# Small VectorE results in PSUM, and fills issued earlier, in the first stage of a four-layer kernel

## The reference

```python
# x = x + tanh(g_xattn[0]) * mix(layernorm(x), ctx, ctx, Wt, Wp, Wg, Wz, gamma, beta)
t = einsum('oc,bcd->bod', Wt, inp_v)          # inp_v = ctx
p = einsum('oc,bcd->bod', Wp, inp_q)          # inp_q = layernorm(x)
g = einsum('oc,bcd->bod', Wg, inp_k)          # inp_k = ctx
att = einsum('bgcd,bgcd->bg', pg, gg) * 0.125 # one number per batch row and group of 16 channels
x = einsum('goc,bgcd->bgod', Wz, att * tg)
xn = (x - mean) / sqrt(var + EPS)             # over the 16 channels and 256 columns of a group
return xn * gamma + beta + inp_v
```

## Time and profile before

| | us |
|---|---|
| median of 3 runs | 1526.99 (1524.5 to 1534.19) |
| the profiled execution | 1540.32 |
| its span, first to last instruction | 1538.4 |
| mix, to the last instruction of VectorE in it | 170.0 |

### The profile page before, as it was taken

One profiled execution on the slowest core, in us unless ns is written; L12 is line 12 of the kernel. 1 busy time (PEld: TensorE's weight loads), 2 busy tenths in 40 slices (PEclk: granted clock), 3 DMA queues, 4 the chain that ended last, 5 costly groups with the idle time before them and its releaser, 6 DMA issues. The chain is left out here.

```text
span 1538.4 us, 28073 instructions
## 1 busy us (share of the span) xinstructions
PE 1209.9 (79%) x9258; PEld 1100.5 (72%) x9258; DVE 945.9 (61%) x2119; ACT 784.5 (51%) x2201; POOL 514.5 (33%) x579
## 2 busy tenths in 40 slices
PE   3767316999789999999999999974888767778674
PEld 2555215889689998888888888874787666677664
DVE  4888684545366666568766877764866322234666
ACT  3555203555366667666766656553654433345442
POOL 4433233564100001100255005542525555554442
PEclk8676557999899999999999999987899878789997
DMA  3349753553500000000133003423845545444886
GB/s 89 122 126 277 189 113 122 158 145 84 144 8 15 8 1 22 29 8 1 45 118 115 15 1 128 135 90 126 264 129 150 158 138 152 138 128 142 274 278 219
DMA packets 139522, 177.12 MB, mean 115 GB/s; under 512 B 21984, under 2 KB 120448, under 8 KB 139392
## 3 DMA queue, kind: packets, MB, share of 16 engines
q1 hardware_dynamic: 110928, 122.62, 27.8%
q0 software_dynamic: 17792, 43.14, 8.7%
q10 hardware_dynamic: 10672, 9.65, 2.2%
HBM read 107.28 MB, written 68.09 MB: 114 GB/s over the span
## 5 line engine op out<-in xcount | busy, mean ns | idle before, releaser
L1617 ACT ACTIVATE attend_s<-attend_s,attend_less 128x128 f32<-128x128 f32 x512 | 198.4, 392 | 108.6 <-DVE attend_less L1758 102.0
L2268 POOL DMA_INDIRECT answers<-moe_yb,moe_dst x160 | 157.3, 983 | 195.8 <-ACT moe_yb L2347 83.9
L1572 POOL TENSOR_TENSOR router_xn<-rest_acc,router_mv 128x512 f32<-128x512 f32 x12 | 12.5, 1043 | 424.9 <-DVE router_rs L1232 371.2
L82 PE MATMUL moe_psU<-moe_wl,moe_xh 128*128 (+1 forms) x384 | 119.8, 312 | 3.3 <-issue 3.3
L83 PE MATMUL moe_psU<-moe_wh,moe_xh 128*128 (+1 forms) x384 | 120.0, 312 | 2.9 <-issue 2.9
L81 PE MATMUL moe_psU<-moe_wh,moe_xl 128*128 (+1 forms) x384 | 121.0, 315 | 1.5 <-issue 1.5
L2414 DVE TENSOR_TENSOR moe_it<-moe_it,moe_psU 128x256 f32<-128x256 f32 x96 | 40.2, 419 | 130.8 <-ACT moe_it L2329 76.9
L1635 ACT ACTIVATE attend_pt<-attend_psS 128x1024 f32<-128x1024 f32 x64 | 65.5, 1024 | 85.0 <-PE attend_psS L1909 80.8
L2577 PE MATMUL moe_psI<-const_ident,moe_it 128*128 128x128 f32 x192 | 41.6, 301 | 85.3 <-DVE moe_il L2410 77.5
L1200 POOL DMA_INDIRECT slots<-router_row,router_idx x80 | 81.1, 1013 | 79.3 <-DMA router_row<-normed_rows 58.2
L1756 DVE SCALAR_TENSOR_TENSOR attend_s<-attend_psS,held_bias 128x1024 f32<-128x1024 f32 x64 | 78.0, 1219 | 44.4 <-PE attend_psS L1902 44.3
(11 more groups left out here) (386 smaller groups left out, 4240.8 us busy)
## 6 DMA issues: line engine op xcount, KB each, us to landing
moe_xg<-slots SPq DMA_DIRECT2D x160, 129.0 KB
moe_both<-answers SPq DMA_DIRECT2D x28, 512.0 KB
router_row<-normed_rows SPq DMA_DIRECT2D x40, 256.0 KB
slots<-mix_zero SPq DMA_DIRECT2D x4, 2048.0 KB, 17.7
layer_raw<-in_wi_dram SPq DMA_DIRECT2D x8, 1024.0 KB, 5.0
layer_raw<-in_wo_dram SPq DMA_DIRECT2D x8, 1024.0 KB, 6.8
moe_raw<-in_gex_dram SPq DMA_DIRECT2D x17, 384.0 KB
moe_both<-normed_rows SPq DMA_DIRECT2D x24, 256.0 KB
```

What stands on the lines that cost most here:

```text
L82: pe.matmul(out, wh, ml, start=False, stop=False)
L1617: last = nc.scalar.activation(s[:, g, j, :], s[:, g, j, :], ACT.Exp, bias=less[:, g, j:j + 1], accum_out=sm[:, g, j:j + 1])
L2268: nc.gpsimd.indirect_dma_start(out=R.YT[q], out_offset=bass.IndirectOffsetOnAxis(ap=dst[:, r % NM, s:s + 1], axis=0), in_=yb[:, r % NY, s, ...
```

## The change

- psS, a bank of PSUM of which the group sums take 12 columns, gives room to four more small results: mv2 (columns 16 to 23), ps1 and ps2 (24 to 31). `sums` names the 12 columns of group sums.
- Each instruction of the chain L431 to L442 that read two SBUF operands now reads one from PSUM (`sums`, ps1 or ps2) and one from SBUF. Their number and their order are as before, and the copy into s3 (L430) stays. The reciprocal goes to a tile of its own, sdr.
- mv2 is in PSUM: L457 writes it there, L341 (ScalarE) and L461 read it.
- SyncE's loop is written out, and behind the loads of the third step stand the two stores of zeros, and behind those of the third to sixth step one fill pair each. The wait for the fills stays at the end.

```diff
@@ names
+        sdr = sb("sdr", [P, NB])
-        mv2 = sb("mv2", [P, NB, 2])
+        sums = psS[:, 0:3 * NB].rearrange("p (a b) -> p a b", b=NB)
+        mv2 = psS[:, 4 * NB:6 * NB].rearrange("p (a b) -> p a b", b=2)
+        ps1, ps2 = (psS[:, k * NB:(k + 1) * NB] for k in (6, 7))
@@ SyncE
-            with sp.Fori(0, STEPS // 2) as h:
-                front(h * 2, 0, h)
-                front(h * 2 + 1, 1, h)
-            sp.wait_ge(zeros_up, 1)
-            sp.dma_start(X2[DUMMY:ROWS, :], zero[:]).then_inc(dummies, 16)
-            sp.dma_start(XN[DUMMY:ROWS, :], zero[:]).then_inc(dummies, 16)
-            kept.sync(sp, zero[:])
+            for n in range(STEPS):
+                front(n, n % 2, n // 2)
+                if n == 2:
+                    sp.wait_ge(zeros_up, 1)
+                    sp.dma_start(X2[DUMMY:ROWS, :], zero[:]).then_inc(dummies, 16)
+                    sp.dma_start(XN[DUMMY:ROWS, :], zero[:]).then_inc(dummies, 16)
+                if 2 <= n < 6:
+                    kept.sync(sp, zero[:], (n - 2) // 2, n % 2)
+            kept.synced(sp)
             sp.wait_ge(dummies, 32)
@@ VectorE, back
-                c(nc.vector.tensor_copy(s3[:], psS[:, 0:3 * NB].rearrange("p (a b) -> p a b", b=NB)))
-                nc.vector.scalar_tensor_tensor(t1[:], s3[:, 0, :], 4.0, s3[:, 0, :], ALU.mult, ALU.mult)
-                c(nc.vector.tensor_tensor(t2[:], s3[:, 1, :], s3[:, 1, :], ALU.mult))
-                c(nc.vector.tensor_tensor(t2[:], s3[:, 2, :], t2[:], ALU.subtract))
-                nc.vector.tensor_tensor(va[:], t1[:], t2[:], ALU.mult).then_inc(va_ready, 1)
+                c(nc.vector.tensor_copy(s3[:], sums))
+                nc.vector.scalar_tensor_tensor(ps1, sums[:, 0, :], 4.0, s3[:, 0, :], ALU.mult, ALU.mult)
+                c(nc.vector.tensor_tensor(t2[:], sums[:, 1, :], s3[:, 1, :], ALU.mult))
+                c(nc.vector.tensor_tensor(t2[:], sums[:, 2, :], t2[:], ALU.subtract))
+                nc.vector.tensor_tensor(va[:], ps1, t2[:], ALU.mult).then_inc(va_ready, 1)
                 dve.wait_ge(sdu_ready, n + 1)
-                c(nc.vector.reciprocal(t1[:], sdu[:]))
-                c(nc.vector.scalar_tensor_tensor(t2[:], s3[:, 0, :], 2.0, t1[:], ALU.mult, ALU.mult))
+                c(nc.vector.reciprocal(sdr[:], sdu[:]))
+                c(nc.vector.scalar_tensor_tensor(ps2, sums[:, 0, :], 2.0, sdr[:], ALU.mult, ALU.mult))
                 if isinstance(n, int) and n == 0:
                     dve.wait_ge(gbt_up, 2)
-                c(nc.vector.tensor_scalar(ab[:, 0, :], t2[:], gbt[:, 0:1], None, ALU.mult))
-                c(nc.vector.tensor_tensor(t1[:], ab[:, 0, :], s3[:, 1, :], ALU.mult))
-                nc.vector.tensor_scalar(ab[:, 1, :], t1[:], -1.0, gbt[:, 1:2], ALU.mult, ALU.add).then_inc(ab_ready, 1)
+                c(nc.vector.tensor_scalar(ab[:, 0, :], ps2, gbt[:, 0:1], None, ALU.mult))
+                c(nc.vector.tensor_tensor(ps1, sums[:, 1, :], ab[:, 0, :], ALU.mult))
+                nc.vector.tensor_scalar(ab[:, 1, :], ps1, -1.0, gbt[:, 1:2], ALU.mult, ALU.add).then_inc(ab_ready, 1)
@@ Sorted
-    def sync(self, sp, zero):
+    def sync(self, sp, zero, q, kind):
 
         sp.wait_ge(self.spare_up, 2)
-        for q in range(2):
-            heads = ...
-            spare = ...
-            for kind, rows_ in enumerate((heads, spare)):
-                sp.dma_start(rows_[:, :, 0:D], zero.unsqueeze(1).to_broadcast([P, E1, D])).then_inc(self.spare_in, 16)
-                sp.dma_start(rows_[:, :, D:WIDE], self.marks[:, q, kind]).then_inc(self.spare_in, 16)
+        if kind == 0:
+            rows_ = ...
+        else:
+            rows_ = ...
+        sp.dma_start(rows_[:, :, 0:D], zero.unsqueeze(1).to_broadcast([P, E1, D])).then_inc(self.spare_in, 16)
+        sp.dma_start(rows_[:, :, D:WIDE], self.marks[:, q, kind]).then_inc(self.spare_in, 16)
+
+    def synced(self, sp):
         sp.wait_ge(self.spare_in, 128)
```

More of the change, by code:

```diff
@@ L1099, in gpsimd @@
         last.then_inc(self.spare_up, 1)
-    def sync(self, sp, zero):
+    def sync(self, sp, zero, q, kind):
         sp.wait_ge(self.spare_up, 2)
-        for q in range(2):
-            heads = self.XS[q][0:E1 * REGION[q], :].rearrange("(t r) n -> r t n", r=REGION[q])[0:P]
-            spare = self.XS[q][E1 * REGION[q] + P:E1 * (REGION[q] + P) + P, :].rearrange("(t p) n -> p t n", p=P)
-            for kind, rows_ in enumerate((heads, spare)):
-                sp.dma_start(rows_[:, :, 0:D], zero.unsqueeze(1).to_broadcast([P, E1, D])).then_inc(self.spare_in, 16)
-                sp.dma_start(rows_[:, :, D:WIDE], self.marks[:, q, kind]).then_inc(self.spare_in, 16)
+        if kind == 0:
+            rows_ = self.XS[q][0:E1 * REGION[q], :].rearrange("(t r) n -> r t n", r=REGION[q])[0:P]
+        else:
+            rows_ = self.XS[q][E1 * REGION[q] + P:E1 * (REGION[q] + P) + P, :].rearrange("(t p) n -> p t n", p=P)
+        sp.dma_start(rows_[:, :, 0:D], zero.unsqueeze(1).to_broadcast([P, E1, D])).then_inc(self.spare_in, 16)
+        sp.dma_start(rows_[:, :, D:WIDE], self.marks[:, q, kind]).then_inc(self.spare_in, 16)
+    def synced(self, sp):
         sp.wait_ge(self.spare_in, 128)
```

## The result

The changed kernel takes 1513.42 us (median of 4 runs, 1511.57 to 1514.90), the one before 1528.23 on the same chip: a ratio of 0.990, interval 0.986 to 0.993. Measured once more beside later kernels, it gives 0.988, interval 0.986 to 0.990 (1518.16 against 1537.78 us). By these ratios the saving is 15.4 and 18.5 us, a little over 1%. The forecast was 13.4 us, to 1513.6.

A forecast was written before the change was run, and what follows sets the result against it. VectorE, fullest in mix, was held 23.4 us by GpSimd; 10 go into waits for L315 and L518. Seven periods sum to 109.0 against 122.3 us; fills 0: 1527.0 - 13.4 = 1513.6 us, range 1505 to 1521.

The forecast's parts named there:

- The hold and what frees it: Mix, VectorE: L461, L437 and L434 wait for GpSimd; one PSUM operand each ends it, 23.4 us off VectorE's time.
- No surcharge for PSUM: VectorE reading or writing PSUM in mix: 0 us taken, at most 1.3 us for writes at L457 over seven steps.
- What is late next: In mix without the holds, L349 waits for L315 on ScalarE, and L404 on VectorE for the logits of L518.
- The size of the chain: Mix period: 4.91 + 9.13 + 0.03 + 1.74 = 15.8 us, the seventh 14.1; 13.4 us less in all.
- the clock rises: Rival, 15%: TensorE idles less in shorter mix steps and its clock rises; up to 6 us beyond, 1507.5 us.
- its bound by w: At 2.4 GHz in mix, w binds: 4.91 + 10.4 = 15.3 us a step against 15.8; transposes may give 0.5 more.
- the prediction's own signs: Mix: L450 every 15.8 us, with waits for L315 and L518, means right; periods of 14.5 or 17.9 mean wrong.
- Fills: SyncE's early fills in mix: worth 0 alone or with part one, 9.5 or 6 us from being waited for.
- part one: Moving one operand of each held VectorE instruction in mix to PSUM: 13.4 us less.
- The slower rival: Rival, 4%: early fills on SyncE make mix's loads late; 1583 us if fill and marks hold the queue 45 us.
- the held L440: Rival, 12%: L440 and L442 in mix are held in place of L437; 6.9 us saved, 1520 us.
- frees nothing: Rival, 6%: a PSUM operand does not free the held VectorE instructions in mix; 1527 us.

The follow-up runs named there:

- The part experiments: Kernel before with only mv2 in PSUM: 0.993, mix 9.5 us sooner; with only the chain's operands in PSUM, fills late: 0.996, mix 4.5 us sooner.
- the MEMSET experiment: Kernel before, GpSimd's z addition replaced by a 4-column sum and a MEMSET of the other 1020: L461 takes 0.16 us, mix ends at 158.5 us.
- first profile: First trace of the changed kernel, no further edit: median 1513.42 us, mix ends at 151.4 us.
- second profile: Changed kernel measured once more, no edit: ratio 0.988 to the kernel before, mix ends at 152.4 us.
- The filler: Changed kernel plus eight unused TensorE transposes before those of xn, in seven steps: 0.986, mix ends at 150.7 us; on the kernel before: 0.999, 170.6 us.

## Why the prediction was right, and where its terms were off

- **The total: right, and closer than it deserved.** 1513.42 us lies in the range of 1505 to 1521, 0.2 from the 1513.6 forecast. That closeness is luck. Mix was 17.6 to 18.6 us shorter and not 13.4, while the first medians, with an interval of 10 to 21 us, differ by 14.8.
- **The hold and what frees it: right.** 23.4 us of VectorE's busy time were waiting behind GpSimd, and one PSUM operand in each ends it. The single row of evidence used, L421 passing where L424 is held, carried to SCALAR_TENSOR_TENSOR and TENSOR_TENSOR. The part experiments show it operand by operand, and the MEMSET experiment points to GpSimd's reads. "SBUF — State Buffer" of the Trainium skill, section "Who interferes with whom", says that a VectorE instruction with two SBUF inputs contends with a GpSimd instruction that reads SBUF, and not with one that only writes it. Every run here agrees, with 1.8 to 2.3 us against 0.16. The held COPY L424 and x_norm read one tensor only; no row shows in which mode they ran.
- **No surcharge for PSUM: right within 0.01 us.** 162 ns for L466 with one PSUM source; 170 with a PSUM output; 165 for 158 at the aggregation into PSUM. ScalarE's root of mv2 even fell from 0.297 to 0.264 us. The figures of "VectorE: DVE Perf Modes" of the Trainium skill, section on the TRN2 errata, 62 cycles more for a PSUM source, do not show in these instructions: 162 ns (L466) with one PSUM source, 163 with none (L431 in the kernel before).
- **What is late next: right in kind.** xn waits for the gs copy, VectorE for the logits, by 0.5 to 1.3 us in the first profile. Moving either wait away showed both to be real: 2 to 3 us for the logits, 3 more for gs once it stood in idle time.
- **The size of the chain: this is the term that failed.** The prediction counted 9.13 us from xn to the end of the logits, the mean of two steps. Seven periods were forecast at 108.9 us (109.0 rounded) and came to 103.3. From x1 to xn: 4.78 us for 4.91, 0.9 in all. From xn to the logits copy: 8.60 us on average in the first six for 9.16, 3.4 in all, and 7.29 for 8.88 in the last, 1.6. From the logits copy to x1: 1.62 for 1.74, 0.7; but 1.0 lost in the last period, where w was then late. Together 5.6 us, 5.0 of them between xn and the logits copy. In the second profile it is 4.5 us, 2.7 of them there.
- **What made that stretch shorter: TensorE's clock.** The granted clock was 1.00 (2.4 GHz) from 87 to 90 us, for 0.51 in the earlier trace rows. A set of transposes takes 0.66 us for 1.11, and in the first profile 11 of 14 sets do so, for 4 of 14 before. The 16 logits matmuls take 3.58 us at the low level and come to 2.44 to 3.59 in the first profile, 3.00 to 3.58 in the second, 3.58 throughout before. Before the set at 87.45 us TensorE idled 1.64 us, for 2.96 before the corresponding one in the kernel before. The filler raised the level as this reading asks. The rival "the clock rises", given 15%, was in the main what happened, and its bound by w, up to 6 us beyond, was well placed. By the prediction's own signs the periods are in between: 15.8 us was to show it right and 14.5 wrong, and the first six are 15.0 on average, 15.2 in the second profile, with the waits where it had them.
- **It was read as a separate case, though the forecast itself brought it about.** Shorter steps mean less idling, and the argument stood in the text. In the trace of the kernel before, the first set of transposes already ran at 0.66 us in four of the seven periods, and a value between would have been the better choice for the sum.
- **Fills: right alone, wrong on top of part one.** "Still 6 us apart" used 13.4 us for the end of mix and 46.7 for the fills; it was 18 and 52.1, and with the fills left late they landed 2.3 us after the last logits copy. Moving them is worth 3 to 4 us of the 18.
- **The slower rival, the held L440, and "frees nothing": all refuted.** L445 takes 222 ns in all eight steps. No load was waited for: the one issued at 71.36 us was used at 88.37, 17.0 us later, near the 19 forecast. SyncE's marks took up to 7.3 us to issue, in time in which it had nothing else to do.

What stays open: what exactly of TensorE's past work decides its level in a step, since equal steps differ (2.79 and 3.58 us for the same 16 logits matmuls), and since the idle time just before is not enough to tell. In the first step of the changed kernel the transposes came 0.36 us after other matmuls and took 1.12 us, at a granted clock of 0.50 that those matmuls had too (38.0 to 41.3 us); in the kernel before, a set ran at 0.66 us after 2.99 us of idling. Also open is how much of the spread in the total after mix is chance.

## What to carry to other kernels

A short instruction with a long duration may be a held one: compare its end with the ends of GpSimd's instructions before pricing the work in it. If it is held and reads two SBUF operands, give it a PSUM operand if one is at hand. Then price the gain along the chain, not on the engine: of 23.4 us off VectorE, 18 reached the end, and each part alone brought only 4.5 and 9.5, since the holds that were left grew or met other instructions and some of the gain came only with both parts. And when steps get shorter, ask again what has so far been hidden with room to spare, here the fills, and what had been slow from idling, here TensorE.

## What the hardware showed that was not expected

- A faster clock on TensorE gave nothing in the kernel before (170.6 us for 170.0), where GpSimd's subtraction then met earlier instructions of VectorE's chain.
- A row of four TENSOR_SCALAR instructions of 256 elements (x_norm), SBUF to SBUF, is held as well, in the run with the logits copied later: up to 1.92 us for 1.38 when GpSimd's reading instruction is still running at its start.
- The same 8 MB of fills needed 46.7 us beside steps of 17.9 us and 52.1 beside steps of 15.1.
